# One attention and mixture-of-experts kernel: row maxima ahead of casts and statistics, a GELU ahead of two weighings, and the last sums taken chunk by chunk

## The chip, the core and the metric

The kernel runs on one core of a Trainium2 chip. Its engines are named as the profile names them: PE (TensorE matmul; PEld is its weight load), DVE (VectorE), ACT (ScalarE), POOL (GpSimd) and SP (SyncE, which here only starts transfers). Each engine works through its own queue in order, and semaphores tie the queues together. The metric is the device time of one execution in microseconds (us); less is better.

## The reference, cut to what matters

```python
x = x + layernorm(attention(layernorm(x), wq, wk, wv, wo))     # x: 4 x 256 x 256 float32
x = x + layernorm(experts(layernorm(x), router, gate_up, down))

def attention(x):          # 16 heads of 128
    q, k = rope(x @ wq), rope(x @ wk);  v = x @ wv
    p = softmax(q @ k.T / 128 - 1e30 * (i < j))
    return sum over heads of (p @ v) @ wo

def experts(x):            # 1024 tokens, 16 experts, 4 of them for each token
    logits = x @ router_weight.T + router_bias
    weights = softmax of the 4 largest logits, 0 elsewhere
    gate, up = (x @ gate_up_proj[e] + bias)[::2], [1::2]
    gate, up = min(gate, 7), clip(up, -7, 7)
    out_e = ((up + 1) * gate * sigmoid(1.702 * gate)) @ down_proj[e] + down_bias[e]
    return sum over experts of weights[:, e] * out_e
```

## The kernel before

**Attention.** There are 64 slots n = 16b + h, one for each batch b (0 to 3) and head h (0 to 15). Every engine's queue is written out by hand as a loop over n. In iteration n PE computes the q and k of slot n + 4 (`qk_chunk`, twelve products, L1457), transposes the probabilities of slot n (`turn_prob`, L1527), computes the scores of slot n + 2 (`scores`, L1518 and L1519), half of the values of a pair of heads (`v_half`), the output projection of slot n - 1 (`output_rows`, L1457 with wo), and then probabilities times values of slot n (`weigh_values`, L1537). There is one bank for scores, so `scores(n + 3)` waits for `row_max(n + 2)`.

DVE in iteration n does, in this order: `oT_low(n - 1)` (L1057), `normalise_prob(n + 1)` (L1048, L1051), side work, `row_max(n + 2)` (L1040, L1042: adds the mask, writes scaled scores and each row's bias for the exponential), `cosine(n + 4)` (L1024) and `rotate(n + 4)` (L1032). The side work depends on b and h: in batch 0 a cast of a head's output weights (`high_o`, L1207) in all iterations but the last; statistics of x (`row_stats`, L1005 to L1012) at n = 5, 10 and 28; the low part of the next batch's transposed x (`xT_low`, L1017) at h = 10; in batches 1 to 3 statistics and residual of the batch before at h = 1 and 2, the router's choice at h = 6 (`choose`), its shares and places at h = 7; and in batch 3 a plan of the early expert tiles at h = 8, 9 and 10 (`count_early`, `plan_early`, `leave_out_early`, L1138 to L1167).

ACT in iteration n swaps the halves of q and k (`swap`, two copies to by_sin), copies the transposed probabilities out (`probT_out`), does its own side work, then `softmax_exp(n + 2)` (L723), which waits for `row_max(n + 2)`, and `oT_high(n)`. POOL multiplies the swapped halves by the sine (`times_sine`, L551) and, in batch 0, computes low parts of weights (L536): `low_qk`, `low_v` in every second iteration, and `low_o(h + 1)`, which waits for DVE's cast of the same head.

**Experts.** Tokens are sorted to 47 tiles of 128 rows. The first 9 tiles (0 to 8) are planned from batches 0 to 2 and run while the last batch is routed; the table of the others is ready later, and SP then loads their rows (`load_rows`, L473) once all rows have been scattered. Per tile: transpose (L1663), gate and up products (L1679), `clamp` on DVE (L1224, L1230), `gelu` on ACT (L811), `gated` on DVE (L1240), the down product on PE (`down`, L1698), `weigh` on ACT (L829; L824 for the last three tiles). ACT's order at the boundary is gelu(7), weigh(6), weigh(7), gelu(8), expert weights of tile 9 (`place_gu`), `xgT_out(9)`. Rows are added to two sums in DRAM by POOL's indirect transfers, but for the last three tiles ("late"), whose rows are added on PE by one-hot products (`add_late`, L1824).

**The end.** For each of four chunks u (two row tiles each) `pe` adds the late tiles j = 0, 1, 2 and the two sums read back from DRAM (`add_sum`, L1830; the two are first added on DVE for u = 0, 1 and on POOL for u = 2, 3, L1418 and L692). DVE then takes statistics (`moe_stats`, L1005 to L1012), ACT centres (L979), POOL computes the reciprocal root (`root`, L523), DVE multiplies and adds x (`finish`, L1435), and SP or ACT writes out. After the last instruction each engine drains and they meet (L51).

Of the kernel before, what the change touches and what calls it, by code (L numbers as in the profile page):

```python
# [28 lines left out]
SLOTS = B * H  # L29
# [6 lines left out]
TILE_MAX = (N * TOP + E * (P - 1)) // P  # L36
# [5 lines left out]
XG, XT, AR, YR, SUMS, LATE = 14, 2, 3, 8, 2, 3  # L42
# [5 lines left out]
def block_kernel(nc, x_d, wq_d, wk_d, wv_d, wo_d, rw_d, rb_d, gu_d, gub_d, dn_d, dnb_d,  # L48
                 rope_cos_d, rope_sin_d, mask_d, ident_d, out_d):
    ctx = ExitStack()  # L50
    with ctx:  # L51
# [127 lines left out]
        sum_a = sb("sum_a", [P, TILES, M])  # L179
# [67 lines left out]
        pe_sum = sem("pe_sum")  # L247
# [266 lines left out]
        def _(pool):  # L514
# [170 lines left out]
            for i in range(EARLY, LAST):  # L685
                add_rows(i)

            for u in (2, 3):
                pool.wait_ge(dma_first[u], 16)
                pool.wait_ge(dma_second[u], 16)  # L690
                tiles = slice(2 * u, 2 * u + 2)
                pool.tensor_tensor(sum_a[:, tiles, :], sum_a[:, tiles, :], sum_b[:, tiles, :], ALU.add).then_inc(two[u], 1)  # L692

            for u in range(4):
                root("moe", u)


# [1 line left out]
        def _(sc):  # L699
# [107 lines left out]
            def gelu(i):  # L807
                sc.wait_ge(dve_gate, i + 1)
                if i >= 2:
                    sc.wait_ge(dve_act, i - 1)  # L810
                sc.activation(glu[:, i % 2, :, :], gate[:, i % 2, :, :], ACT.Gelu_apprx_sigmoid).then_inc(act_glu, 1)  # L811
# [9 lines left out]
            def weigh(i, e):  # L821
                sc.wait_ge(pe_y, i + 1)
                if i >= LAST:
                    sc.activation(late_h[:, i - LAST, :], ps_out[i][:, 0:M], ACT.Copy,  # L824
                                  scale=xg[:, i % XG, bass.ds(e + M, 1)]).then_inc(act_y, 1)
                    return
                if i >= YR:
                    sc.wait_ge(dma_sum[HOME[i - YR]], added(i - YR))
                sc.activation(y[:, i % YR, :], ps_out[i][:, 0:M], ACT.Copy,  # L829
                              scale=xg[:, i % XG, bass.ds(e + M, 1)]).then_inc(act_y, 1)  # L830
# [120 lines left out]
            weigh(5, experts[5])  # L951
            start_out(B - 1)
            gelu(7)
            weigh(6, experts[6])
            weigh(7, experts[7])
            gelu(8)
            sc.wait_ge(dve_table, 1)
            experts[EARLY] = place_gu(EARLY)
            xgT_out(EARLY)
# [29 lines left out]
        def _(dve):  # L989
# [45 lines left out]
            def row_max(n):  # L1035

                dve.wait_ge(pe_s, n + 1)
                if n >= 2:
                    dve.wait_ge(act_exp, n - 1)
                dve.memset(row_sum[:, n % 2, :], 0.0)  # L1040
                for i, (lo, hi) in enumerate([(0, P), (P, P + T)]):
                    m = dve.tensor_tensor_reduce(score[:, n % 2, lo:hi], ps_s[:, lo:hi], mask[:, P:T] if i == 0 else mask[:, :],  # L1042
                                                 -1.0 / D, FILL, ALU.add, ALU.min, row_bias[:, n % 2, i:i + 1])
                m.then_inc(dve_max, 1)

            def normalise_prob(n):
                dve.wait_ge(act_exp, n + 1)
                dve.reciprocal(row_rec[:, n % 2, :], row_sum[:, n % 2, :]).then_inc(dve_rec, 1)  # L1048
                dve.wait_ge(dve_rec, n + 1)
                for i, (lo, hi) in enumerate([(0, P), (P, P + T)]):  # L1050
                    m = dve.tensor_scalar(prob[:, n % 2, lo:hi], prob[:, n % 2, lo:hi], row_rec[:, n % 2, i:i + 1],  # L1051
                                          None, ALU.mult)
                m.then_inc(dve_norm, 1)
# [237 lines left out]
            for n in range(SLOTS - 3):  # L1291
                b, h = n // H, n % H
                if n >= 1:
                    oT_low(n - 1)
                if n >= 1:
                    normalise_prob(n + 1)
                if b == 0:
                    if h + 1 < H:
                        high_o(h + 1)
                    if h == 5:  # L1300
                        small_tables()
                if n in X_SLOTS:
                    u = X_SLOTS.index(n) + 1
                    dve.wait_ge(dma_x[u], 16)
                    row_stats(x, "x", u)
                if b >= 1:
                    if h == 1:
                        attn_stats(b - 1)
                    if h == 2:
                        residual(b - 1)  # L1310
                    if h == 6:
                        choose(b - 1)
                    if h == 7:
                        share(b - 1)
                        place(b - 1)
                if b == B - 1:
                    if h == 8:
                        count_early()
                    if h == 9:
                        plan_early()  # L1320
                    if h == 10:
                        leave_out_early()
                if b < B - 1 and h == 10:
                    xT_low(b + 1, ps_spare[b])
                if n + 2 < SLOTS:
                    row_max(n + 2)
                if n + LEAD < SLOTS:
                    cosine(n + LEAD)
                    rotate(n + LEAD)
# [90 lines left out]
            def moe_stats(u):  # L1420

                dve.wait_ge(pe_sum, u + 1)
                row_stats(ps_sum[u][:, :].rearrange("p (s m) -> p s m", s=2), "moe", u, 0)

            def finish(u):

                n = NORMS.index(("moe", u))
                dve.wait_ge(pool_rstd, n + 1)
                if u < B - 1:
                    dve.wait_ge(pool_x, 2 * u + 2)  # L1430
                else:
                    dve.wait_ge(act_x, 1)
                for i in range(2):
                    dve.wait_ge(act_moe, 2 * u + i + 1)
                    dve.scalar_tensor_tensor(out=sum_b[:, 2 * u + i, :], in0=sum_b[:, 2 * u + i, :],  # L1435
                                             scalar=rstd[:, 2 * n + i:2 * n + i + 1], in1=x[:, 2 * u + i, :],
                                             op0=ALU.mult, op1=ALU.add).then_inc(dve_out, 1)
# [4 lines left out]
            moe_stats(1)  # L1442
            finish(0)
            moe_stats(2)
            moe_stats(3)
            finish(1)
            finish(2)
            finish(3)

# [2 lines left out]
        def _(pe):  # L1452
# [232 lines left out]
            def down(i):  # L1685

                e = pe.value_load(entry(i, 0), min_val=0, max_val=E - 1)
                pe.wait_ge(dve_act, i + 1)
                if i == TILE_MAX - 1:
                    pe.wait_ge(dve_up, i)  # L1690
                elif i == 1:
                    pe.wait_ge(dve_up, 3)
                elif i >= 2:
                    pe.wait_ge(act_y, i - 1)
                    if i - 2 >= LAST:
                        pe.wait_ge(dve_late, i - 1 - LAST)
                for r in range(2):
                    m = pe.matmul(ps_out[i][:, 0:M], act[:, i % AR, r, :],  # L1698
                                  dn_w[:, bass.ds(e, 1), r, :].rearrange("p o m -> p (o m)"),
                                  start=(r == 0), stop=(r == 1))  # L1700
                m.then_inc(pe_y, 1)
# [116 lines left out]
            def add_late(u, j, first=False):  # L1818

                pe.wait_ge(dve_turn, 4 * j + u + 1)  # L1820
                pe.wait_ge(dve_late, j + 1)
                for s in range(2):
                    for rows in (late_h, late_l):
                        pe.matmul(ps_sum[u][:, s * M:(s + 1) * M], turn[:, j, 2 * u + s, :], rows[:, j, :],  # L1824
                                  start=first and s == 0 and rows is late_h, stop=False, skip_group_check=True)

            def add_sum(u, rows, last=False):

                for s in range(2):
                    m = pe.matmul(ps_sum[u][:, s * M:(s + 1) * M], ident[:, :], rows[:, 2 * u + s, :], start=False,  # L1830
                                  stop=last and s == 1, skip_group_check=True)
                return m

            pe.wait_ge(act_xgT, TILE_MAX)
            for u in range(4):
                add_late(u, 0, first=True)
            down(TILE_MAX - 1)
            for u in range(4):
                add_late(u, 1)
            for u in range(3):  # L1840
                add_late(u, LATE - 1)
                pe.wait_ge(two[u], 1)
                add_sum(u, sum_a, last=True).then_inc(pe_sum, 1)
            add_late(3, LATE - 1)
            pe.wait_ge(two[3], 1)
            add_sum(3, sum_a, last=True).then_inc(pe_sum, 1)


# [35 lines left out]
```

## Time and profile before

| | |
|---|---|
| Median of three runs | 482.07 us (482.01 to 483.24) |
| The profiled execution's own time | 482.69 us |
| Its span, from first to last instruction | 480.6 us |
| PE busy | 463.5 us, 96% of the span |
| PEld, DVE, ACT, POOL busy | 437.0, 365.4, 323.9, 246.1 us |
| Granted TensorE clock, mean | 0.996 |
| SP sees the last output landed | at 478.9 us of the span |

A row of the timeline is: start in us, length in us, engine, line, operation, tile written <- tiles read, shape, count, and in brackets the idle time of the engine before it with what ended it. Neighbouring instructions of one kind are merged to one row. The end of a matmul is modelled, so PE can look busy for 0.2 us or so while it stands; the distance between the starts of two equal products in successive iterations tells more.

### The profile page before, as it was taken

What the parts mean: (1) busy time and instruction counts of PE and PEld (TensorE: products, weight loads), DVE (VectorE), ACT (ScalarE), POOL (GpSimd) and SP (SyncE); (2) the same over time, 40 slices, a digit from 0 to 9 for tenths busy, and PEclk for the clock granted to TensorE, in tenths of its full rate; (3) what the DMA queues carried; (4) which work ended last, traced back from release to release, by engine and by line L of the source; (5) the groups of instructions that cost most, each with busy time, mean ns of one, the idle gap of its engine ahead of it and who ended that gap; (6) DMA issues with size and microseconds to landing.
All of it is one profiled execution on the core that took longest, in us unless ns stands there. A gap on an engine that the chain in (4) does not pass through costs nothing. (4 is left out here: it accounts for less than half of the span.)

```text
span 480.6 us, 11719 instructions
## 1 busy us (share of the span) xinstructions
PE 463.5 (96%) x3480; PEld 437.0 (91%) x3480; DVE 365.4 (76%) x1271; ACT 323.9 (67%) x809; POOL 246.1 (51%) x232
## 2 busy tenths in 40 slices
PE   8999999999999999999999999999999999999992
PEld 5889998999999999999999998888889999999992
DVE  5999888687777678687569599758856788877766
ACT  5878977767677777668677766678456565655622
POOL 1887985435223246435354226402875666666514
PEclk9999999999999999999999999999999999999998
DMA  7478651999400000000264645550277667675462
GB/s 205 134 241 277 206 184 38 373 369 369 142 1 1 23 14 38 26 26 27 70 233 167 212 160 182 180 166 27 87 148 119 112 118 116 111 125 70 47 196 87
DMA packets 61677, 65.25 MB, mean 136 GB/s; under 512 B 4977, under 2 KB 56497, under 8 KB 61617
## 3 DMA queue, kind: packets, MB, share of 16 engines
q1 hardware_dynamic: 52880, 53.30, 34.9%
q0 software_dynamic: 7872, 10.49, 13.0%
q10 hardware_dynamic: 864, 0.72, 0.5%
q8 instruction: 29, 0.48, 0.4%
q14 instruction: 32, 0.25, 0.2%
HBM read 31.58 MB, written 32.92 MB: 134 GB/s over the span
## 5 line engine op out<-in xcount | busy, mean ns | idle before, releaser
L551 POOL TENSOR_TENSOR by_sin<-by_sin,rope_sin 128x512 f32<-128x512 f32 x64 | 82.6, 1290 | 141.7 <-ACT by_sin L701 131.2
L701 ACT ACTIVATE by_sin<-bank 64x512 f32<-64x512 f32 x128 | 75.8, 592 | 34.2 <-PE bank L1457 32.6
L1457 PE MATMUL bank<-xT_parts,qk_h 128*128 128x256 f32 x504 | 98.3, 293 | 0.3 <-DVE qk_l L1198 0.3
L1679 PE MATMUL bank<-xgT,gu_now 128*128 128x128 f32 x752 | 92.3, 276 | 0.2
L652 POOL DMA_INDIRECT sum_d<-y,xg x44 | 69.2, 1572 | 39.5 <-DMA sum_d<-y,xg 17.8
L1679 PEld LDWEIGHTS bank<-xgT,gu_now 128*128 128x128 f32 x752 | 87.8, 192 | 1.7 <-issue 1.0
L1457 PEld LDWEIGHTS bank<-xT_parts,qk_h 128*128 128x128 f32 x504 | 78.0, 191 | 1.0 <-DVE qk_l L1198 0.5
L723 ACT ACTIVATE prob<-score,row_bias 128x128 f32<-128x128 f32 (+1 forms) x128 | 57.0, 449 | 29.7 <-DVE row_bias L1042 29.7
L1457 PE MATMUL bank<-xT_parts,qk_l 128*128 128x256 f32 x252 | 71.3, 283 | 0.0
L1457 PE MATMUL bank<-wv_h,xT_parts 128*128 128x256 f32 x256 | 67.3, 326 | 0.0
L1032 DVE TENSOR_TENSOR qkT<-bank,by_sin 128x512 f32<-128x512 f32 x64 | 44.2, 691 | 14.8 <-POOL by_sin L551 12.3
L1042 DVE CUSTOM_DVE_ANT_0 score<-bank,mask 128x128 f32<-128x128 f32 (+1 forms) x128 | 40.4, 352 | 17.9 <-issue 17.7
L1698 PE MATMUL bank<-dn_w,act 128*128 x188 | 48.5, 381 | 1.1 <-DVE act L1240 1.1
L1457 PEld LDWEIGHTS bank<-xT_parts,qk_l 128*128 128x128 f32 x252 | 48.0, 190 | 0.0
L811 ACT ACTIVATE glu<-gate 128x256 f32<-128x256 f32 x47 | 19.6, 416 | 39.6 <-DVE gate L1224 39.3
L1057 DVE TENSOR_TENSOR oT_l<-bank,oT_h 128x256 fp32r<-128x256 f32 x64 | 27.1, 424 | 24.8 <-ACT oT_h L701 24.8
L1051 DVE TENSOR_SCALAR prob<-prob,row_rec 128x128 f32<-128x128 f32 (+1 forms) x128 | 44.2, 388 | 2.3
L1457 PEld LDWEIGHTS bank<-wv_h,xT_parts 128*128 128x128 f32 x256 | 43.9, 189 | 1.6
L1024 DVE TENSOR_TENSOR bank<-bank,rope_cos 128x512 f32<-128x512 f32 x64 | 44.4, 693 | 0.7 <-ACT by_sin L701 0.6
L1224 DVE TENSOR_SCALAR gate<-bank,gate_bias 128x128 f32<-128x128 f32 x94 | 28.7, 346 | 15.8 <-PE bank L1679 15.2
L554 POOL DMA_INDIRECT rows_d<-xrow,slot_of x32 | 32.8, 1025 | 14.6 <-DVE slot_of L1133 8.3
L1537 PE MATMUL bank<-probT,V 128*128 128x256 f32 x126 | 38.8, 389 | 1.0 <-ACT probT L701 0.9
(203 smaller groups left out, 1068.1 us busy)
## 6 DMA issues: line engine op xcount, KB each, us to landing
rows_d<-blank SPq DMA_DIRECT2D x32, 576.0 KB, 7.3
gu_w<-_L_ffn_gate_up_proj_dram SPq DMA_DIRECT2D x16, 512.0 KB, 4.2
xg<-rows_d SPq DMA_DIRECT2D x47, 144.0 KB, 2.5
dn_w<-in_L_ffn_down_proj_dram SPq DMA_DIRECT2D x16, 256.0 KB, 4.3
raw_qk<-in_L_attn_wq_dram SPq DMA_DIRECT2D x16, 128.0 KB, 3.5
raw_qk<-in_L_attn_wk_dram SPq DMA_DIRECT2D x16, 128.0 KB, 3.5
raw_v<-in_L_attn_wv_dram SPq DMA_DIRECT2D x8, 256.0 KB, 2.7
raw_o<-in_L_attn_wo_dram SPq DMA_DIRECT2D x16, 128.0 KB, 2.5
```

What stands on the lines that cost most here:

```text
L551: pool.tensor_tensor(v, v, rope_sin[:, :].unsqueeze(1).broadcast_to([P, 2, T]), ALU.mult).then_inc(pool_sin, 1)
L652: pool.indirect_dma_start(out=sum_d[HOME[i]], out_offset=bass.IndirectOffsetOnAxis(ap=xg[:, i % XG, TOKEN:TOKEN + 1].bitcast(U32), axis=0) ...
L701: return sc.activation(out, in_, ACT.Copy)
L723: e = sc.activation(prob[:, n % 2, lo:hi], score[:, n % 2, lo:hi], ACT.Exp, bias=row_bias[:, n % 2, i:i + 1], scale=-1.0, accum_out=row_su ...
L1024: dve.tensor_tensor(v, v, rope_cos[:, :].unsqueeze(1).broadcast_to([P, 2, T]), ALU.mult).then_inc(dve_cos, 1)
L1032: dve.tensor_tensor(qkT[:, n % QR, :, :].rearrange("p w t -> p (w t)"), ps_qk[n][:, :], by_sin[:, n % 2, :], ALU.add).then_inc(dve_rope, 1)
L1042: m = dve.tensor_tensor_reduce(score[:, n % 2, lo:hi], ps_s[:, lo:hi], mask[:, P:T] if i == 0 else mask[:, :], -1.0 / D, FILL, ALU.add, AL ...
L1051: m = dve.tensor_scalar(prob[:, n % 2, lo:hi], prob[:, n % 2, lo:hi], row_rec[:, n % 2, i:i + 1], None, ALU.mult)
L1457: m = pe.matmul(out, lhs, rhs, start=first and i == 0, stop=last and i == len(terms) - 1, skip_group_check=not (first and last))
L1537: pe.matmul(ps_oT[n][:, 0:T], V[:, v, 0, a * D:(a + 1) * D], turned[n][:, 0:T], start=True, stop=False, skip_group_check=True)
L1679: m = pe.matmul(ps_gu[i][:, (2 * s + r) * P:(2 * s + r + 1) * P], gu_now[:, i % 2, k, s, r * P:(r + 1) * P], xgT[:, i % XT, k, :], start=( ...
L1698: m = pe.matmul(ps_out[i][:, 0:M], act[:, i % AR, r, :], dn_w[:, bass.ds(e, 1), r, :].rearrange("p o m -> p (o m)"), start=(r == 0), stop= ...
```

## The change

Four edits in the order of queues; no instruction is added or removed.

```diff
@@ gpsimd, after the last add_rows @@
-            for u in (2, 3):
+            def add_two(u):
                 pool.wait_ge(dma_first[u], 16)
                 pool.wait_ge(dma_second[u], 16)
                 tiles = slice(2 * u, 2 * u + 2)
                 pool.tensor_tensor(sum_a[:, tiles, :], ...).then_inc(two[u], 1)
-            for u in range(4):
+            add_two(2)
+            root("moe", 0)
+            add_two(3)
+            for u in range(1, 4):
                 root("moe", u)
@@ scalar, at the boundary of early and other tiles @@
             gelu(7)
+            gelu(8)
             weigh(6, experts[6])
             weigh(7, experts[7])
-            gelu(8)
             sc.wait_ge(dve_table, 1)
@@ vector, loop over slots @@
                 if n >= 1:
                     normalise_prob(n + 1)
+                if n + 2 < SLOTS:
+                    row_max(n + 2)
                 if b == 0:
                     if h + 1 < H:
                         high_o(h + 1)
...
                     xT_low(b + 1, ps_spare[b])
-                if n + 2 < SLOTS:
-                    row_max(n + 2)
                 if n + LEAD < SLOTS:
                     cosine(n + LEAD)
                     rotate(n + LEAD)
@@ vector, the end @@
             moe_stats(1)
             finish(0)
             moe_stats(2)
+            finish(1)
             moe_stats(3)
-            finish(1)
             finish(2)
             finish(3)
@@ tensor, the end @@
             pe.wait_ge(act_xgT, TILE_MAX)
+            add_late(0, 0, first=True)
+            add_late(1, 0, first=True)
+            down(TILE_MAX - 1)
+            add_late(2, 0, first=True)
+            add_late(3, 0, first=True)
+            add_late(0, 1)
+            add_late(1, 1)
             for u in range(4):
-                add_late(u, 0, first=True)
-            down(TILE_MAX - 1)
-            for u in range(4):
-                add_late(u, 1)
-            for u in range(3):
+                if u >= 2:
+                    add_late(u, 1)
                 add_late(u, LATE - 1)
                 pe.wait_ge(two[u], 1)
                 add_sum(u, sum_a, last=True).then_inc(pe_sum, 1)
-            add_late(3, LATE - 1)
-            pe.wait_ge(two[3], 1)
-            add_sum(3, sum_a, last=True).then_inc(pe_sum, 1)
```

## Rows read from the trace of the kernel before

**Rows 1.** PE's timeline: score products in six stretches, and one product that waits.

```profile
25.18 0.46 PE L1518 MATMUL bank<-qkT 128*128 128x128 f32 x2 [1.22 <-DVE row_bias L1042]
...
34.63 0.46 PE L1518 MATMUL bank<-qkT 128*128 128x128 f32 x2
...
40.08 0.39 PE L1518 MATMUL bank<-qkT 128*128 128x128 f32 x2
...
73.57 0.46 PE L1518 MATMUL bank<-qkT 128*128 128x128 f32 x2 [0.66 <-DVE row_bias L1042]
...
76.50 0.70 PE L1537 MATMUL bank<-probT,V 128*128 128x256 f32 x2 [0.31 <-ACT probT L701]
...
79.02 0.39 PE L1518 MATMUL bank<-qkT 128*128 128x128 f32 x2
...
83.51 0.39 PE L1518 MATMUL bank<-qkT 128*128 128x128 f32 x2
...
291.55 0.44 PE L1518 MATMUL bank<-qkT 128*128 128x128 f32 x2
...
297.04 0.46 PE L1518 MATMUL bank<-qkT 128*128 128x128 f32 x2
```

**Rows 2.** DVE's timeline in attention: two casts, two low parts, a small product.

```profile
32.55 1.38 DVE L1207 CAST wo_h<-raw_o 128x256 fp32r<-128x256 f32 x1
...
64.77 0.28 DVE L1207 CAST wo_h<-raw_o 128x256 fp32r<-128x256 f32 x1
...
68.14 0.42 DVE L1057 TENSOR_TENSOR oT_l<-bank,oT_h 128x256 fp32r<-128x256 f32 x1 [1.09 <-ACT oT_h L701]
...
74.74 0.42 DVE L1057 TENSOR_TENSOR oT_l<-bank,oT_h 128x256 fp32r<-128x256 f32 x1
...
294.04 1.23 DVE L1150 TENSOR_TENSOR skipped<-passed,skip 128x16 f32<-128x16 f32 x1
```

**Rows 3.** POOL's timeline beside the first cast of rows 2.

```profile
32.43 1.35 POOL L551 TENSOR_TENSOR by_sin<-by_sin,rope_sin 128x512 f32<-128x512 f32 x1
```

**Rows 4.** Batch 3, h = 6 and 7: end of DVE's choice, PE's product that needs it.

```profile
278.54 1.20 DVE L1108 TENSOR_TENSOR earlier<-earlier,chosen 128x16 f32<-128x16 f32 x1
```

**Rows 5.** PE's timeline, the product that needs it.

```profile
281.77 0.29 PE L1613 MATMUL bank<-earlier,ones 128*128 128x16 f32 x2
```

**Rows 6.** The boundary of the expert tiles, ACT's timeline.

```profile
349.84 0.47 ACT L829 ACTIVATE y<-bank,xg 128x256 f32<-128x256 f32 x1 [0.39 <-PE bank L1698]
350.21 0.41 ACT L811 ACTIVATE glu<-gate 128x256 f32<-128x256 f32 x1
```

**Rows 7.** The same stretch, PE's timeline.

```profile
351.22 1.13 PE L1698 MATMUL bank<-dn_w,act 128*128 x4 [1.07 <-DVE act L1240]
352.18 0.38 PE L1663 MATMUL bank<-ident,xg 128*128 128x128 f32 x2
```

**Rows 8.** SP's row loads in 346 to 354, and their landing times (the line's view).

```profile
348.59 3.22 SPq L473 DMA_DIRECT2D xg<-rows_d  x3
...
DMA to landing us min/median/max: 2.7/2.9/3.1
```

**Rows 9.** The end, POOL's timeline.

```profile
467.99 2.50 POOL L692 TENSOR_TENSOR sum_a<-sum_a,sum_b 128x512 f32<-128x512 f32 x2 [9.12 <-DMA sum_b<-sum_d]
470.44 1.39 POOL L523 TENSOR_TENSOR rstd<-var_eps,minus_half 128x2 f32<-128x2 f32 x2
...
474.40 0.92 POOL L523 TENSOR_TENSOR rstd<-var_eps,minus_half 128x2 f32<-128x2 f32 x1 [0.46 <-DVE var_eps L1011]
```

**Rows 10.** The end, DVE's timeline.

```profile
468.75 0.54 DVE L1011 TENSOR_SCALAR var_eps<-mean_var 128x2 f32<-128x2 f32 x1
...
471.20 0.88 DVE L1435 SCALAR_TENSOR_TENSOR sum_b<-sum_b,rstd,x 128x256 f32<-128x256 f32 x2 [0.62 <-POOL rstd L523]
...
474.15 0.17 DVE L1011 TENSOR_SCALAR var_eps<-mean_var 128x2 f32<-128x2 f32 x1
```

**Rows 11.** The view of line 51, where each engine ends (duration in ns, start in us).

```profile
L51 POOLq DRAIN  x1: 5953/5953/5953, 474.4 to 474.4; - x1
```

## The prediction

> **What bounds the kernel now.** The page comes first: PE is busy 463.5 of 480.6 us at full clock, so the time is PE's work plus the places where PE stands. The waits of PE name DVE's row maxima, ACT's transposed probabilities and a down product. The distance between score products then prices them: where nothing disturbs it is 83.51 - 79.02 = 4.49 us [rows 1]. Four stretches are longer.
>
> - Slots 1 to 5. The score product at 25.18 stands 1.22 us, and 34.63 to 40.08 takes 5.45, 0.96 too much [rows 1].
> - Slots 10 and 11. The product at 73.57 stands 0.66 and the next interval, 73.57 to 79.02, is again 5.45, 0.96 too much; 0.31 of it is the value product at 76.50, which waits for ACT [rows 1].
> - Batch 3, h = 8 to 10. 291.55 to 297.04 takes 5.49 [rows 1]; it holds two small transposes more, so I count 0.8 as lost. The iteration after it has the same side work on DVE and gets the same price, 0.9.
> - The boundary of the expert tiles: `down(8)` stands 1.07 for its operand [rows 7].
>
> From 354 to 461 PE never waits, and what it gains before is carried to the end. The last 13 us are a chain through DMA, POOL and DVE.
>
> **Part 1: row maxima first.** In the three attention stretches DVE reached `row_max` late because something stood ahead of it: a cast of 1.38 us that takes 0.28 elsewhere [rows 2], statistics and `xT_low` (about 1.9 us), or the plan of the early tiles. The cast is long because POOL's by_sin runs from 32.43 to 33.78 and the cast ends when that ends [rows 2, 3]; in the plan the product at 294.04 takes 1.23 for 16 columns for the same reason [rows 2]. A row maximum takes 0.6 us and is not held, so put first it fills time in which DVE stood anyway: the first stretch and the plan gain there up to 0.6 us of DVE time in each iteration, and ACT's exponentials start 0.6 to 2.5 us sooner.
>
> What is late next. DVE's work in an iteration is unchanged, and `oT_low` still comes after `rotate`. At slot 10 DVE is busy without a gap from 68.14 to 75.16 and `oT_low(10)` starts at 74.74 [rows 2]; PE's output product needs it, so of the 0.66 + 0.96 only the wait for ACT goes, since ACT's copies no longer queue behind a late exponential: 0.3 to 0.5 us, taken as 0.5. In slots 1 to 5 the held casts give DVE about 0.5 us twice, and ACT is nearly full there: of 1.22 + 0.96 (about 2.7 with the shorter delays behind them) I take 1.0. In batch 3 the held products give DVE 0.6, 0.8 and 0.8 us in three iterations, and PE's losses of 0.1, 0.8 and 0.9 can go nearly all: I take 1.2. Together **2.7 us**; bounds 0 (each wait comes back one step on) and 6.3 (2.7 + 1.8 + 1.8, all gone).
>
> Costs. In batches 1 to 3 `row_max` now waits for its scores (DVE already does, up to 0.9 us) and side work queues behind it. The tightest user is the router: `earlier` ends at 278.54 + 1.20 = 279.74, one more step to 279.95, and PE needs it at 281.77 [rows 4, 5], 1.8 us later. The choice starts 1.4 us later (0.8 of waiting, 0.6 of maxima) but its own held product (1.20 for 16 columns) gets free, so it ends 0.5 to 1.4 later: nothing. In batch 0 the cast now starts when by_sin has just started, and is held up to 1.1 us more in every second iteration. In those DVE has 1.09 us of idle time before `oT_low` [rows 2], and POOL's low parts are ready more than 1 us before use: nothing, but with little left.
>
> **Part 2: gelu(8) ahead of two weighings.** gelu(8) starts at 350.21, behind weigh(7), which waits for a down product [rows 6]; its gate values are ready at 348.87 by DVE's timeline. Moved, it ends at about 349.35, DVE's product (0.42, after up at 349.38) at 349.85, and `down(8)` can start at 350.0 instead of 351.22 [rows 7]. Then the next wait shows: `turn_tile(9)`, at 352.18 before [rows 7], needs rows that SP loads at 348.59 and that land after 2.7 us at the least, at 351.3 [rows 8]. So 352.18 becomes 351.35: 0.85, and a little less waiting for weights behind it. The two weighings are 0.3 to 0.5 later, and nobody waits for them but POOL's additions, which are behind by order. I take **0.9 us**; bounds 0.5 and 1.2. SP's loads hang on the scatters, not on this edit.
>
> **Part 3: the end.** `down(46)` starts some 0.7 us sooner, for it stood behind 16 products of 0.12 us and stands behind 8. This brings late_low to 465.0, but the first `add_two` needs the sum from DRAM, landed 2.6 us after its issue at 462.67; so chunk 0's statistics start at 467.3 instead of 467.73: 0.45 us. There the gain stops. POOL's addition of chunk 2 begins at 467.99 [rows 9], fixed by the same DMA, and var_eps(0), 0.17 us alone at 474.15, takes 0.54 at 468.75 and ends when POOL's addition ends [rows 10]. In the new kernel it arrives at 468.3, is held to the same 469.28, and root(0) runs 469.3 to 470.0. Then POOL adds chunk 3, 1.25 us to 471.25 (470.49 before), and DVE's var_eps(1), ready at 470.3, is held until then, with `finish(0)` behind it: 471.3 against 471.20 [rows 10]. After it come statistics (1.15), finish(1) (0.8, moved), statistics (1.15): root(3) starts 0.1 + 0.8 = 0.9 us later than 474.40 [rows 9]. The last `finish` ends only 0.1 to 0.3 later.
>
> Which of these sets the end? SP sees the last output at 478.9, but POOL's drain runs to 474.37 + 5.95 = 480.32 [rows 11], 5.0 us after root(3) ends (475.32, [rows 9]). On DVE the drain ends with the last work. I read POOL's drain as a fixed 5 us behind its last instruction, so root(3) sets the end: 0.9. If it hung on the output transfers, 0.3. I take **0.8 us lost**; bounds 0.9 lost and 1.0 gained (root(0) really lets finish(0) start at 470.0, and the drain follows).
>
> The product of 16 columns held for 1.23 us at 294.04 shows that DVE and POOL exclude each other when both read from SBUF [rows 2]. The Trainium skill says so in "SBUF — State Buffer", section "Who interferes with whom": a DVE instruction with two SBUF inputs contends with a GpSimd instruction that reads SBUF, and whoever issues first has the pair for the whole instruction. It speaks against this edit, since finish(0) has two such inputs and POOL's addition follows root(0) at once; by the rule finish(0) waits to 471.25 even if var_eps(1) were early, without it the end gains about 1.0.
>
> **Sum.** 2.7 + 0.9 - 0.8 = 2.8 us. The profiled execution took 482.69, so 479.9; it was 0.6 above the median of the runs (482.07), so **479.3 us**.
>
> **Rivals.**
>
> - *Handed on.* DVE and ACT bound the disturbed stretches, so each stall returns at the next product; for it speaks DVE's gapless 68 to 75, against it the DVE time that stood idle under POOL. Attention 0.6, boundary 0.6, end -0.9: 0.3 us, 481.8.
> - *All goes.* Attention 4 (of 6.3), boundary 1.0, or the forecast with the end at +1.0: 4.5 us, 477.6. For it: exponentials come up to 2.5 us sooner. Against: held var_eps.
> - *Maxima wait for scores.* The edit moves DVE's idle time, not the maxima, and the router's choice is late: forecast less 1.5, 480.8. Against: in the disturbed stretches the scores are ready long before.
> - *Slower: the cast is held twice.* In batch 0, in the six iterations with `low_v`, the cast falls behind by_sin and then behind the low part of the values, 2.6 us. The 1.09 of idle time is gone and 1.2 us remain each: 6 x 1.2 = 7.2 lost against 2.8 gained, 486.5. It decides from the point at which the hold exceeds 1.1 us. Against it: between two POOL instructions one DVE instruction has always got through.
>
> **Chances.** Forecast 0.50 (own range 478.2 to 480.5), handed on 0.17, all goes 0.18, maxima wait 0.08, slower 0.07. The range 477.3 to 481.9 leaves out the slower rival and the edges. 0.3% is 1.45 us, about what a measurement tells from no change. Faster by more: 0.48 of the forecast, 0.18, 0.02, or 0.68. Within: 0.02, 0.15, 0.05, or 0.22. Slower: 0.10.
>
> **What would show it.** The score products at 25.18 and 73.57 no longer wait on row_bias; the distances 34.63 to 40.08 and 291.55 to 297.04 shrink by 0.5 and more; batch 0's casts have more of the 1.4 us kind; an output product waits for oT_l near 75. `down(8)` follows the filler products, and turn_tile(9) waits for xg. At the end var_eps(0) and var_eps(1) are both long, and POOL's drain starts 0.9 later against the last row load. It is wrong if PE waits on qk_l, wv_l or prob in batch 0, or if the drain's end does not follow root(3).

## The result, and the profile of the changed kernel

| | before | after |
|---|---|---|
| Median of six runs each | 482.29 us (482.01 to 483.94) | 479.76 us (478.35 to 481.17) |
| The profiled execution's own time | 482.69 us | 480.23 us |
| Its span | 480.6 us | 478.1 us |
| PE / DVE / POOL busy | 463.5 / 365.4 / 246.1 us | 462.7 / 364.8 / 248.2 us |
| SP sees the last output | 478.9 us | 475.7 us |

The ratio of the runs is 0.9933, with a 95% interval of 0.9913 to 0.9953. It is not the quotient of the two medians, which is 0.9948 and lies in the interval too: the medians say 2.5 us less, the ratio 3.2. The predicted time was 479.3 us.

In the page, the group of exponentials shows the stall that went: 9.0 us of idle time for row_bias, where it was 29.7. Columns: busy us, mean ns, idle us before it and what ended most of it.

```profile
L727 ACT ACTIVATE prob<-score,row_bias 128x128 f32<-128x128 f32 (+1 forms) x128 | 57.0, 449 | 9.2 <-DVE row_bias L1046 9.0
```

Lines of PE, DVE and ACT are four higher than before. PE's timeline, the products of [rows 1] and those that now wait:

```profile
24.16 0.46 PE L1522 MATMUL bank<-qkT 128*128 128x128 f32 x2 [0.35 <-DVE row_bias L1046]
...
33.83 0.39 PE L1522 MATMUL bank<-qkT 128*128 128x128 f32 x2
...
39.08 0.39 PE L1522 MATMUL bank<-qkT 128*128 128x128 f32 x2
...
72.48 0.39 PE L1522 MATMUL bank<-qkT 128*128 128x128 f32 x2
...
74.86 0.39 PE L1461 MATMUL bank<-wo_h,oT_h 128*128 128x256 f32 x1 [0.85 <-DVE oT_l L1061]
...
290.50 0.39 PE L1522 MATMUL bank<-qkT 128*128 128x128 f32 x2
...
295.22 0.39 PE L1522 MATMUL bank<-qkT 128*128 128x128 f32 x2
```

The wait of 1.22 at slot 3 is 0.35, and that at slot 13 is gone; in its place the output product waits 0.85 for oT_l. 290.50 to 295.22 is 4.72, where 5.49 stood. But 33.83 to 39.08 is still 5.25, where 5.45 stood: 0.2 less, and the prediction had named 0.5 and more as its sign. DVE's timeline, the instructions of [rows 2] and two that answer to them:

```profile
30.25 2.67 DVE L1055 TENSOR_SCALAR prob<-prob,row_rec 128x128 f32<-128x128 f32 x2
...
45.66 1.16 DVE L1211 CAST wo_h<-raw_o 128x256 fp32r<-128x256 f32 x1
...
48.02 0.66 DVE L1015 TENSOR_SCALAR var_eps<-mean_var 128x2 f32<-128x2 f32 x1
...
74.39 0.41 DVE L1061 TENSOR_TENSOR oT_l<-bank,oT_h 128x256 fp32r<-128x256 f32 x1
...
293.15 0.17 DVE L1154 TENSOR_TENSOR skipped<-passed,skip 128x16 f32<-128x16 f32 x1
```

The cast at 45.66 is of the held kind and the product of 16 columns, 1.23 before, takes 0.17. The two products of `normalise_prob` at 30.25, 0.55 together elsewhere, are held as well; in the page the mean of all 128 of them is 417 ns, where it was 388. The boundary of the expert tiles, PE's timeline ([rows 7]):

```profile
347.78 1.13 PE L1702 MATMUL bank<-dn_w,act 128*128 x4
348.74 0.38 PE L1667 MATMUL bank<-ident,xg 128*128 128x128 f32 x2
...
352.57 2.02 PE L1683 MATMUL bank<-xgT,gu_now 128*128 128x128 f32 x16 [0.24 <-ACT xgT L705]
```

`down(8)` (347.78) no longer waits, and neither does `turn_tile(9)` (348.74), for which the prediction had named a wait for xg.

The end, POOL's and then DVE's timeline ([rows 9, 10]), and the view of the line where the engines end ([rows 11]; duration in ns, start in us):

```profile
464.65 1.27 POOL L693 TENSOR_TENSOR sum_a<-sum_a,sum_b 128x512 f32<-128x512 f32 x1 [8.85 <-DMA sum_b<-sum_d]
466.03 0.72 POOL L523 TENSOR_TENSOR rstd<-var_eps,minus_half 128x2 f32<-128x2 f32 x1
466.73 1.27 POOL L693 TENSOR_TENSOR sum_a<-sum_a,sum_b 128x512 f32<-128x512 f32 x1
...
472.00 0.92 POOL L523 TENSOR_TENSOR rstd<-var_eps,minus_half 128x2 f32<-128x2 f32 x1 [1.02 <-DVE var_eps L1015]
```

```profile
465.22 0.73 DVE L1015 TENSOR_SCALAR var_eps<-mean_var 128x2 f32<-128x2 f32 x1
...
466.93 1.10 DVE L1015 TENSOR_SCALAR var_eps<-mean_var 128x2 f32<-128x2 f32 x1
...
468.01 0.87 DVE L1439 SCALAR_TENSOR_TENSOR sum_b<-sum_b,rstd,x 128x256 f32<-128x256 f32 x2
```

```profile
L51 POOLq DRAIN  x1: 5953/5953/5953, 472.0 to 472.0; - x1
...
L51 SPq COMPARE_BRANCH  x1: 38/38/38, 475.7 to 475.7; - x1
```

Both var_eps end where an addition of POOL ends (465.92 and 468.00), and finish(0) starts at once behind the second.

### The profile page after: what moved, and what is told of

Same layout as the page of the kernel before. It is cut to its first block, busy times and chain, and to the rows that moved or that the text cites. A ratio compares the mean times of both kernels' runs of the same rounds, so it can differ in the third digit from the quotient of the medians.

```text
span 478.1 us, 11720 instructions
## 1 busy us (share of the span) xinstructions
PE 462.7 (97%) x3480; PEld 437.1 (91%) x3480; DVE 364.8 (76%) x1271; ACT 324.6 (68%) x809; POOL 248.2 (52%) x232
## 4 chain that ended last, share of the span: by engine, by line
PE 78%; DVE 3%; ACT 1%; issue 1%; POOL 0%; POOLq 0%; DVEq 0%; ACTq 0%
PE bank L1461 29%; PE bank L1683 17%; PE bank L1702 8%; PE bank L1541 5%; PE bank L1523 4%; PE bank L1531 3%; PE bank L1543 2%; PE bank L1522 2%; PE bank L1667 2%; PE bank L1647 1%; PE bank L1602 1%; PE bank L1828 1%; DVE stats L1009 1%; PE bank L1566 1%; ACT prob L727 0%
## 5 line engine op out<-in xcount | busy, mean ns | idle before, releaser
L1055 DVE TENSOR_SCALAR prob<-prob,row_rec 128x128 f32<-128x128 f32 (+1 forms) x128 | 47.8, 417 | 2.3
L1228 DVE TENSOR_SCALAR gate<-bank,gate_bias 128x128 f32<-128x128 f32 x94 | 28.7, 346 | 17.5 <-PE bank L1683 14.6
L1461 PE MATMUL bank<-wo_h,oT_h 128*128 128x256 f32 x128 | 36.7, 287 | 2.3 <-DVE oT_l L1061 2.1
```

The lines of the kernel that those rows point to most:

```text
L1461: m = pe.matmul(out, lhs, rhs, start=first and i == 0, stop=last and i == len(terms) - 1, skip_group_check=not (first and last))
```

## The experiments

The executions of one kernel differ by 0.5 to 5 us, so each trace is also read in stretches of PE's own timeline. The slots repeat closely; the last two columns still hold some of that jitter. In us:

| kernel | slots 2 to 3 | slots 8 to 12 | slots 12 to 13 | slots 58 to 61 | tile 5 to 40 | late rows to end |
|---|---|---|---|---|---|---|
| before | 5.34 | 18.51 | 5.32 | 16.80 | 106.75 | 19.24 |
| after | 4.48 | 19.26 | 4.50 | 14.96 | 106.28 | 19.91 |
| maxima alone | 4.47 | 19.22 | 4.49 | 14.96 | 107.11 | 19.18 |
| GELU alone | 5.33 | 19.78 | 5.32 | 16.79 | 105.91 | 18.99 |
| after, old end | 4.46 | 19.22 | 4.49 | 14.96 | 106.01 | 18.97 |
| stats(3) first | 4.46 | 19.24 | 4.50 | 14.96 | 106.32 | 18.71 |
| n = 5 in the old order | 4.45 | 19.72 | 4.50 | 14.96 | 106.29 | 18.99 |
| casts first | 5.33 | 19.28 | 4.50 | 14.96 | 106.47 | 20.85 |

"Slots" are starts of score products, "tile 5 to 40" starts of gate products, 35 tiles across the boundary; "late rows to end" runs from the first `add_late` product to the end of the span. Medians are compared within the group that shared a chip.

### First group: the parts (before: 483.21 us)

**Maxima alone.** Before, with the row maxima moved.

```diff
                     normalise_prob(n + 1)
+                if n + 2 < SLOTS:
+                    row_max(n + 2)
...
-                if n + 2 < SLOTS:
-                    row_max(n + 2)
```

> Only the row maxima are moved; GELU and end as before. Theory (the trace after shows it: score products 2.8 us earlier at slots 61 to 63, 0.2 of that run to run, and 0.2 lost again in the tiles from 325 to 338): PE reaches the boundary of the expert tiles 2.3 to 2.5 us sooner than before, the end passes it on, time 479.9 us, ratio 0.995. Rival 'handed on': the stalls return at the next product, 481.7. Rival 'the gain is really that of GELU and end': 482.3. In the trace the output product waits for oT_l near 50 and 75 us, as it does with all edits, and the distance between the score products at slots 59 to 62 is 4.5 to 4.6.

480.39 us, 2.8 less, ratio 0.9938 (0.9923 to 0.9953). At slots 61 to 63 PE is 2.47 sooner than before: the gain of attention is whole without the other edits, and "handed on" falls. At `down(8)` 2.07 is left, less than expected: PE stands 0.55 at 336.32 for an xgT copy. In nine of the fourteen traces PE stands at that product, in that of before it doesn't. The intervals behind slot 59 are 4.72 and 5.75 (5.50 and 6.69 before), not the 4.5 to 4.6 expected.

**GELU alone.** Before, with gelu(8) ahead of weigh(6) and weigh(7).

> Only gelu(8) is moved. Theory: the wait of down(8), 1.07 before, goes, and 0.3 comes back two tiles on where an xgT copy is late: PE 0.7 to 0.85 us sooner from 355 on, time 481.5. Rival: the boundary only gained because attention had come sooner (or the loads of the rows of tile 9 hold it back at once): 482.3, no change. Rival 'full price', the 1.07 all gone: 481.2.

482.59 us, 0.6 less, ratio 0.999 (0.9972 to 1.0009): the time alone tells nothing. The trace does: `down(8)` no longer waits, and tiles 5 to 40 take 0.84 less than before, although PE stood 0.53 at 339.86 for an xgT copy in that stretch. The twelve traced kernels with this edit take 105.91 to 106.47 there (mean 106.2), the two without it 106.75 and 107.11. Unasked, the run showed something else: slots 8 to 12, where its code is that of before, took 19.78, not 18.51. The rows of n = 5 show a difference. DVE's timeline before, and then here:

```profile
47.61 0.15 DVE L1012 TENSOR_SCALAR minus_mean<-mean_var 128x2 f32<-128x2 f32 x1
```

```profile
47.90 1.27 DVE L1012 TENSOR_SCALAR minus_mean<-mean_var 128x2 f32<-128x2 f32 x1
```

POOL's low part of the values began at 47.63 before, just behind `minus_mean`, and at 47.84 here, just ahead of it: a shift of 0.08 us of one engine against the other goes with 1.1 us of DVE's time.

**After, with the old end** (TensorE's, GpSimd's and VectorE's parts of the end undone).

> Row maxima and GELU as after, the end (TensorE, GpSimd and VectorE) as before. Theory: the new end loses 0.6 us against the work that reaches it (PE was 3.08 us sooner before it, GpSimd's last root 2.4), so this kernel takes 479.8 - 0.6 = 479.2, and root(3) starts 3.1 us sooner than before. Rival 'the new end gains': its chunk-wise sums start 0.45 earlier and without them the time is 480.2 or more.

479.28 us, 3.9 below before, ratio 0.9922 (0.9905 to 0.9938). The stretch to the end is 18.97, 0.94 below that of after.

**Stats(3) first.** After, with one instruction pair moved back.

```diff
             moe_stats(2)
-            finish(1)
             moe_stats(3)
+            finish(1)
```

> After, but VectorE takes the statistics of chunk 3 ahead of finish(1), as before. Theory: GpSimd's last root starts 0.8 us sooner (the two instructions of finish(1), 0.8 us, stood ahead of its statistics), GpSimd's drain of 5.95 us follows it, time 479.0. Rival 'the end hangs on the output transfers or VectorE's last instruction': both move by 0.1 at most, time 479.8 and the drain shrinks or grows.

478.83 us, 4.4 below before, ratio 0.9909 (0.9891 to 0.9928). From POOL's first root to its last it takes 5.17 where after takes 5.97: exactly the 0.8 of finish(1). The other 0.4 of the stretch is the read-back of the sums, which happened to land 0.4 sooner.

### Second group (before: 482.43 us)

**After, once more.**

> The changed kernel once more, beside the three that are compared with it. Theory: old end and new end were never timed together; the median of the kernel with the old end was 3.9 us below before, of the one with stats(3) first 4.4. If the new end loses 0.6 to 0.8 against the old one, as the shifts in the traces say, this kernel lies 3.1 to 3.3 below before (ratio 0.993 to 0.9935). Rival: the end costs nothing, 3.9 below.

480.49 us, only 1.9 below before where 3.1 to 3.3 was expected, ratio 0.9956 (0.9939 to 0.9973). Its profiled execution took 482.75 and shows why single runs scatter. PE's timeline:

```profile
465.22 1.84 PE L1834 MATMUL bank<-sum_a,ident 128*128 128x256 f32 x4 [2.81 <-DVE sum_a L1422]
```

PE stood 2.8 us because the sums read back from DRAM were late. SP began the first read at 457.53, against 454.92 in the trace of after, though PE was 0.76 ahead of it there. With that the end took 23.20.

**All four roots off GpSimd.** On top of "stats(3) first":

```diff
@@ gpsimd @@
             add_two(2)
-            root("moe", 0)
             add_two(3)
-            for u in range(1, 4):
-                root("moe", u)
@@ vector, statistics of the end @@
+            chain(dve.tensor_scalar(var_eps[:, cols], mean_var[:, tiles, 1], EPS, None, ALU.add))
+            dve.reciprocal(var_eps[:, cols], var_eps[:, cols]).then_inc(dve_var, 1)
@@ scalar @@
+            load_table(ACT.Sqrt, 3)
             for u in range(4):
+                root(u)
                 centre(u)
...
+                sc.activation(rstd[:, 2 * n:2 * n + 2], var_eps[:, 2 * n:2 * n + 2], ACT.Sqrt).then_inc(act_root, 1)
```

> After with the statistics of chunk 3 ahead of finish(1), and the four final roots taken off GpSimd: VectorE takes the reciprocal (one more instruction of some 0.15 us a chunk), ACT the square root, its table loaded while it stands idle before the centring. GpSimd's last instruction is the addition of chunk 3, which ended at 467.6 in the kernel before this one in the series. Theory 'GpSimd's drain sets the end and starts with its last instruction': it ends near 473.5 and no longer sets the end; SP's sight of the last output does, 475.3 there plus some 0.3 for the reciprocals, so the span shrinks by 1.2 and the time is 477.6 against 478.8. Rival 'the drain waits for the output transfers or for the other engines': it gets longer than 5.95 and ends 1.4 after the last output as before, time 479.1.

478.65 us, ratio 0.9914 (0.9899 to 0.993). POOL's drain no longer sets the end; POOL's last row, then the view of line 51:

```profile
464.35 2.50 POOL L694 TENSOR_TENSOR sum_a<-sum_a,sum_b 128x512 f32<-128x512 f32 x2 [9.10 <-DMA sum_b<-sum_d]
```

```profile
L51 POOLq DRAIN  x1: 6867/6867/6867, 465.0 to 465.0; - x1
...
L51 SPq COMPARE_BRANCH  x1: 38/38/38, 476.3 to 476.3; - x1
```

The drain ends at 465.0 + 6.87 = 471.9, 5.0 behind the additions (466.85), and waits for no output. But the 1.2 us were not there: DVE's timeline shows that the two additions, now back to back, hold var_eps(0) and minus_mean(0) for 0.99 and 1.11, where "stats(3) first" has 0.47 and 1.09 for var_eps(0) and var_eps(1). With the added reciprocals, DVE's work from the first statistics to the last `finish` takes 10.44 in place of 9.10.

```profile
464.67 0.99 DVE L1022 TENSOR_SCALAR var_eps<-mean_var 128x2 f32<-128x2 f32 x1
465.69 0.17 DVE L1023 RECIPROCAL var_eps<-var_eps 128x2 f32<-128x2 f32 x1
465.77 1.11 DVE L1026 TENSOR_SCALAR minus_mean<-mean_var 128x2 f32<-128x2 f32 x1
```

The reciprocal between them took 0.17, though POOL's second addition ran from 465.59 to 466.86: it was not held.

**n = 5 in the old order.** "Stats(3) first", with `row_max(7)` behind cast and statistics again.

> After with the statistics of chunk 3 ahead of finish(1), and in the one iteration n = 5 the row maxima behind cast and statistics, as before. Theory: 0.7 us of the gain of the first slots was given back at slots 8 to 12, because in n = 5 the cast (1.16 against 0.29) and var_eps (0.66 against 0.19) were held by GpSimd and oT_l came late (output product at 50.52). With the old order there the cast is short again, PE is 0.5 to 0.7 us sooner from slot 12 on and the time 478.2. Rival 'VectorE is simply full': the cast is held elsewhere or the scores of slot 8 wait in place of the output product, no gain, 478.8 or worse.

479.27 us, ratio 0.9931 (0.9917 to 0.9945). My theory fell. In n = 5 the cast is short again (0.28 at 44.91) and so is var_eps, yet slots 8 to 12 take 19.72, 0.5 more than with the new order. The hold had moved on by one instruction, to `minus_mean` on DVE's timeline, which speaks for the rival:

```profile
46.48 1.31 DVE L1016 TENSOR_SCALAR minus_mean<-mean_var 128x2 f32<-128x2 f32 x1
```

**One root more on GpSimd.** After, with a root behind the last one, whose result nobody uses.

> After with one more root instruction on GpSimd behind the last one; nobody uses its result. Theory 'the drain is a fixed 5.95 us behind GpSimd's last instruction': the drain starts 0.7 to 0.9 us later against the last root, is again 5.95 long and the end moves by as much, while SP sees the last output when it did. Rival 'the drain's end hangs on the outputs': it starts later and is shorter by as much.

480.26 us in a single execution. POOL's timeline and the view of line 51:

```profile
471.40 0.92 POOL L523 TENSOR_TENSOR rstd<-var_eps,minus_half 128x2 f32<-128x2 f32 x1 [1.02 <-DVE var_eps L1017]
472.29 0.69 POOL L701 TENSOR_TENSOR minus_half<-var_eps,minus_half 128x2 f32<-128x2 f32 x1
```

```profile
L51 POOLq DRAIN  x1: 6588/6588/6588, 471.4 to 471.4; - x1
...
L51 SPq COMPARE_BRANCH  x1: 38/38/38, 475.1 to 475.1; - x1
```

The drain is listed from 471.4, where the earlier root begins, so its length is not the constant; its end is. It ends at 478.0, 5.0 behind the end of the added root (472.98), as it ended 5.0 behind the last root before and after. The end moves by 0.68 against PE (20.59 in place of 19.91), by the root that nobody needs, while SP sees the last output 17.5 us behind the late rows in both. The first theory holds, with its length of the drain corrected.

### Third group (before: 483.7 us)

**Two roots off GpSimd.** "Stats(3) first", with reciprocal and square root elsewhere only for chunks 2 and 3; roots 0 and 1 stay between and behind the additions.

```diff
             add_two(2)
             root("moe", 0)
             add_two(3)
-            for u in range(1, 4):
-                root("moe", u)
+            root("moe", 1)
```

> After with stats(3) ahead of finish(1), and only the roots of chunks 2 and 3 taken off GpSimd (reciprocal on VectorE, square root on ACT); those of chunks 0 and 1 stay between and behind GpSimd's two additions. With all four gone VectorE lost 1.7 us: var_eps(0) and minus_mean(0) were held for 0.99 and 1.11 us by two additions back to back. Theory: the holds are again those of the kernel with four roots on GpSimd (0.47 and 1.09), VectorE's chain is 0.16 longer, GpSimd's drain ends near 473.7 and SP's sight of the last output, 475.3 + 0.2 = 475.5, sets the end in place of 476.7: 1.2 us less than the kernel with stats(3) first, beside which it runs. Rival: the chain of the outputs grows by as much as the drain is shortened, no gain.

**Stats(3) first, once more**, beside it.

> After with stats(3) ahead of finish(1) once more, as the neighbour of the two-roots kernel and of the cast-first one. Theory: 3.9 to 4.4 below before, as in its first run (0.991); GpSimd's drain sets the end 5.05 us behind the end of its last root. Rival: the 1.2 us between it and the changed kernel, which ran in another call, is chance, and it lies 2.5 to 3 below before.

Two roots off: 478.59 us, ratio 0.991 (0.9889 to 0.9931). Its neighbour: 480.32 us, ratio 0.9931 (0.9913 to 0.995). So 1.7 us between them, but the neighbour's runs reach from 478.89 to 484.21, and its profiled execution had the read-back very late: SP's timeline shows the second read at 463.34, where after has it at 459.63.

```profile
457.15 1.92 SPq L504 DMA_DIRECT2D sum_a<-sum_d  x4
463.34 1.90 SPq L504 DMA_DIRECT2D sum_b<-sum_d  x4
```

PE stands 3.83 us there and the end takes 23.89. In traces with the read-back in time, two roots off takes 18.21 from the late rows to the end and stats(3) first 18.71: 0.5 gained, not 1.2. In the view of line 51 the last output is now what ends last. DVE's timeline has no gap of 0.2 us from its statistics of chunk 0 (463.31) to the end of the last `finish` (473.12):

```profile
L51 POOLq DRAIN  x1: 5962/5962/5962, 467.2 to 467.2; - x1
...
L51 SPq COMPARE_BRANCH  x1: 38/38/38, 475.3 to 475.3; - x1
```

It has the lowest median of the kernels tried, but its interval overlaps those of "all four roots off" (0.9914) and of "stats(3) first" in its first run (0.9909): which of the three is best stays open.

**A smaller addition.** After, with 16 of 256 columns in POOL's addition of chunk 3.

> The changed kernel, but GpSimd's addition of chunk 3 covers 16 of the 256 columns of each tile: the rest of that chunk's second sum is left out. Theory 'var_eps(1) is held by that addition and finish(0) stands behind it': var_eps(1) takes 0.17 in place of 1.10, finish(0) and all that is behind it on VectorE start 0.9 sooner, and GpSimd's last root stands 0.9 less behind its first one (5.97 us from start to start in the changed kernel). Rival 'VectorE waits for root(0) or root(1) anyway, or for PE's sums of chunk 1': the idle time moves to finish(0) and root(3) stays within 0.2.

It leaves out the other 240 columns of that addition. 479.4 us in a single execution. DVE's timeline and POOL's last root:

```profile
467.03 0.17 DVE L1015 TENSOR_SCALAR var_eps<-mean_var 128x2 f32<-128x2 f32 x1
467.11 0.16 DVE L1016 TENSOR_SCALAR minus_mean<-mean_var 128x2 f32<-128x2 f32 x1
467.18 0.87 DVE L1439 SCALAR_TENSOR_TENSOR sum_b<-sum_b,rstd,x 128x256 f32<-128x256 f32 x2
```

```profile
471.16 0.92 POOL L523 TENSOR_TENSOR rstd<-var_eps,minus_half 128x2 f32<-128x2 f32 x1 [1.02 <-DVE var_eps L1015]
```

var_eps(1) takes 0.17 instead of 1.10, finish(0) follows at once, and from first root (465.94) to last it is 5.22 instead of 5.97. The hold of var_eps(1) is shown, at 0.75 of the 0.9 expected. Whether the addition would have held `finish(0)` itself stays open, for no run has it ready while the addition runs.

**Casts first.** After, with the cast of batch 0 ahead of the maxima again, statistics and all else still behind them.

```diff
+                if b == 0 and h + 1 < H:
+                    high_o(h + 1)
                 if n + 2 < SLOTS:
                     row_max(n + 2)
                 if b == 0:
-                    if h + 1 < H:
-                        high_o(h + 1)
```

> The changed kernel, with the row maxima behind the cast in batch 0 as before, but still ahead of statistics, xT_low, the router's choice and the plan. Theory: the cast that was held behind by_sin made the product at 25.18 wait; with it first again the 0.85 us that slot 3 gained are lost, the gains of slots 10 and 11 (0.7) and of batch 3 (1.84) stay: PE at the last score product 0.1 to 0.9 later than in the changed kernel (the 0.75 given back at slots 8 to 12 may go too), time 0.1 to 0.9 above it. Rival 'the maxima ahead of the statistics do all the work': no difference anywhere, and slot 3 gains all the same.

480.76 us, ratio 0.9944 (0.9928 to 0.9961). PE's timeline:

```profile
24.95 0.46 PE L1522 MATMUL bank<-qkT 128*128 128x128 f32 x2 [1.21 <-DVE row_bias L1046]
```

Slots 2 to 3 take 5.33 as before; slots 12 to 13 and 58 to 61 keep the whole gain. PE is 1.01 later than after at the last scores, a little more than the 0.1 to 0.9 expected.

## Why the prediction was right, and where it was right by chance

**Sum.** Forecast 2.8 us less; the medians say 2.53, the profiled pair 2.46, the repeat 1.94. The sum stands on terms of which two were off in opposite directions, so that it came out is in part luck, and it is to be taken apart.

**Part 1, attention: 2.7 forecast, 2.6 found** (PE is 2.77 sooner at slot 61, 0.16 of it before the first changed stretch). The parts:

- *Slots 1 to 5: 1.0 forecast, 0.84 found*. Slot 3 gains 0.86, the interval behind it gives 0.29 back (the output product waits 0.33 at 26.10), and only 0.2 of the 0.96 from 34.63 to 40.08 went. "Casts first" shows that the gain of slot 3 hangs on the order of cast and maximum alone. But 0.73 of it is gone again by slot 12 (0.75 from slot 8 on), in the very cost that I had put at nothing: in batch 0 the casts are held more (0.28 to 1.16, as the text said) and at 50.52 the output product waits 0.27 for oT_l. It is not so simple, though. The old order takes 18.51 in slots 8 to 12 in one trace and 19.78 in another ("GELU alone"), and the old order in n = 5 alone 19.72; the new order takes 19.2 to 19.3 in all ten traces. So the trace of before may have had a lucky stretch, and with two traces of the old order it can't be told what the edit costs there. That the old order is uneven is shown. The rows of `minus_mean` (0.15, 1.27 and 1.31 in those three traces) point to the phase of DVE against POOL; no run sets that phase on purpose.
- *Slots 10 and 11: 0.5 forecast, 0.49 found*, by the mechanism named: 0.82 less in slots 12 to 13, 0.17 and 0.16 given back in the two intervals behind it, and `oT_low(10)` at 74.39 makes the output product wait near 75.
- *Batch 3: 1.2 forecast, 1.84 found*, the mis-sized term. I had listed the losses (0.1, 0.8 and 0.9), wrote that they can go nearly all, and then took a third off for no row. They went entirely, in every kernel with the edit: the exponentials come early and the product of 16 columns is short.
- *Not forecast: 0.17* near slot 26 (5.09 became 4.94 there); no row shows its cause.

With the 0.16 before the first stretch this is 0.16 + 0.84 - 0.73 + 0.49 + 0.17 + 1.84 = 2.77.

**Part 2, boundary: 0.9 forecast.** `down(8)` no longer waits. PE was 2.38 sooner at the gate products of tile 8 and is 3.44 sooner at `turn_tile(9)`, so 1.06 was gained there and not 0.85: the landing of xg, my limit, did not make PE wait in this trace. In the traces of "all four roots off" and "one root more" it did, 0.38 and 0.26. The pair gives 0.47 from tile 5 to 40, the means of all kernels with and without the edit 0.7 (106.2 against 106.9). What was given back was not where I looked. PE stands 0.45 at 336.04 for an xgT copy, ahead of the edit and without it too ("maxima alone": 0.55). Behind the edit ACT's timeline has weigh(8) waiting for a row addition to land, the xgT copy queues behind it, and PE stands at 352.57.

```profile
350.70 0.47 ACT L833 ACTIVATE y<-bank,xg 128x256 f32<-128x256 f32 x1 [1.16 <-DMA sum_d<-y,xg]
```

**Part 3, end: 0.8 lost forecast, 0.67 found in the pair**, 0.8 against the mean of the four traces with the old end (19.10). Each step stood: statistics start 0.45 sooner against PE (464.20 where 467.73 - 3.08 = 464.65 was due), var_eps(0) held to the end of the first addition, root(0), the second addition, var_eps(1) held by it with finish(0) behind, finish(1) 0.8 ahead of the last root. The drain is a constant behind POOL's last instruction, which the added root and the removed roots show from both sides. The prediction put the hold down to both engines reading SBUF, which is too wide, for the reciprocal at 465.69 was not held. By the Trainium skill ("SBUF — State Buffer", section "Who interferes with whom") a DVE instruction with two SBUF inputs contends with a POOL instruction that reads SBUF, and a copy, cast or tensor_scalar can contend with POOL where it runs in a mode that takes both of DVE's ports. var_eps is a tensor_scalar with one input, so it would be the second case. The smaller addition agrees that POOL's instruction holds it: 1.10 became 0.17; which mode it ran in no trace shows.

**The rivals.** "Handed on" and "maxima wait" fall with the maxima alone; "all goes" came true in batch 3 only; "the cast is held twice" never: the longest of the 16 casts took 1.22 us, so one POOL instruction holds it and never a second. What is held by two in a row is `normalise_prob` (2.67 at 30.25), which no rival named.

**Missed.** The end has a second path that PE does not set. The read-back of the sums waits for the row additions to land, and the second read begins between 0.3 us before and 5.1 us after the late rows reach PE. It was in time in most traces; where it was 1.9, 2.4 and 5.1 behind, the end took 20.85, 23.20 and 23.89. In the last two POOL's last row addition had itself begun late, 1.7 and 1.2 us ahead of the late rows, where it is 3.7 to 4.0 ahead in the others; why stays open. The slowest run of the changed kernel (482.75) is one of these; of the others I have no trace, so how much of the scatter from 478.35 on comes from here stays open. It would be the next thing to shorten.

## What to carry to other kernels

Cut the trace into stretches between two events of the bounding engine and compare stretches, not end times: here slots 58 to 61 repeat to 0.01 us while whole executions of one kernel scatter by up to 5 us; the stretches of the tiles and the end scatter more and want several traces. Look at what stands last on every engine, its drain included, and put nothing that could be done earlier or elsewhere ahead of it. And when losses are listed one by one from rows with a single cause, don't take a third off the sum out of caution; put the caution in the range.

## What the runs showed of the hardware

- POOL's drain ends 5.0 us after POOL's last instruction: 475.32 to 480.3 before, 472.98 to 478.0 with the added root, 466.85 to 471.9 without roots, 468.20 to 473.2 with two. In all fourteen traces it is 4.98 to 5.00. The listed length counts from an earlier instruction, so only the end tells; DVE's drain, listed with 0.9 to 1.5 us, ends 0.05 us after DVE's last instruction.
- A tensor_scalar of DVE on 128x2 elements, 0.17 us alone, is held up to 1.1 us by an addition of POOL on 128x512 elements, to that one's end, and two such additions in a row hold two of them. Statistics that read PSUM (0.75 for two) and a reciprocal on 128x2 (0.17) were not held.
